# Attention of an adaLN block: pairs of heads on two row halves of TensorE, or one head at a time with wider score tiles

## What is computed

```python
mod = (silu(c) @ wmod).reshape(8, 6, 1, 1024)
sa, ca, ga, sb, cb, gb = ...                     # ga, gb kept at least 0.25 from zero
h = layernorm(x) * (1 + ca) + sa
x = x + ga * attn(h, W_qkv)                      # 16 heads of 64, 2048 tokens, softmax(q k / 8) v
h = layernorm(x) * (1 + cb) + sb
x = x + gb * ffn(h)                              # 1024 -> 4096 -> 1024, gated by silu
# ffn: activations rounded to 8 bits per token, weights to -1, 0, 1 times their mean magnitude
```

## Time and profile before

| | |
|---|---|
| median of 3 runs (lowest to highest) | 3792.73 us (3792.7 to 3797.2) |
| the profiled execution, its own time | 3794.45 us |
| span of its slowest core (core 6), first to last instruction | 3792.6 us |
| spans of the 8 cores | 3770.1 to 3792.6 us |
| mean granted clock of PE, by core | 0.697 to 0.702 |

### The profile page before, as it was taken

How to read it: one execution, slowest core, us unless ns; L and a number is a source line. 1 busy time by engine, 2 the same in 40 slices (tenths; PEclk the granted TensorE clock), 3 DMA queues, 4 the chain that set the end, 5 groups by cost and what they waited for, 6 DMA issues and landing times.

```text
span 3792.6 us, 31402 instructions; the slowest of 8 cores (3770.1 to 3792.6 us)
## 1 busy us (share of the span) xinstructions
PE 2596.1 (68%) x8072; PEld 767.5 (20%) x8156; DVE 1655.0 (44%) x2454; ACT 1194.3 (31%) x1711; POOL 243.9 (6%) x445
## 2 busy tenths in 40 slices
PE   7528745888888888888888886220856856856856
PEld 1103310111111111111111111010322322322322
DVE  0375642433233344332333443568463463464464
ACT  0100035333344433333444331234342242232232
POOL 0000001100111111100111110000000000000000
PEclk9759855666655666666565666555977977977977
DMA  6349811111111111111211111422414414414413
GB/s 215 147 147 248 247 40 38 51 32 30 40 50 51 50 50 51 39 29 33 50 51 50 50 50 57 145 89 89 145 48 141 125 46 134 124 53 127 132 53 108
DMA packets 209167, 327.47 MB, mean 86 GB/s; under 512 B 135985, under 2 KB 136242, under 8 KB 194658
## 3 DMA queue, kind: packets, MB, share of 16 engines
q1 hardware_dynamic: 167122, 226.88, 19.1%
q0 software_dynamic: 41872, 98.59, 9.7%
HBM read 289.68 MB, written 42.01 MB: 87 GB/s over the span
## 4 chain that ended last, share of the span: by engine, by line
PE 45%; DVE 22%; ACT 12%; DMA 10%; issue 8%; DVEq 1%; ACTq 1%; SPq 0%; POOL 0%; POOLq 0%
PE spsE L734 7%; PE spsO L734 7%; ACT PT L756 5%; PE avps L791 5%; PE avps L787 5%; PE dops L795 5%; PE spsE L746 4%; PE dps L1407 3%; DVE gq L1339 2%; DVE vq L1366 2%; DVE gpb L1243 2%; DVE gup L1256 2%; DVE mab L1269 2%; ACT sgb L1251 2%; DMA wc<-wqkvT 2%
## 5 line engine op out<-in xcount | busy, mean ns | idle before, releaser
L818 DVE RECIPROCAL bcsb<-bcps 128x512 bf16<-128x512 f32 x64 | 214.9, 3357 | 1018.3 <-PE bcps L811 1009.8
L756 ACT ACTIVATE PT<-spsE 128x512 bf16<-128x512 f32 x512 | 305.8, 597 | 411.5 <-PE spsO L746 386.8
L734 PE MATMUL spsE<-c8pair,onesb 1*128 1x512 bf16 x512 | 289.7, 571 | 158.3 <-ACT PT L756 123.8
L1229 PE MATMUL gps<-hA,tg 128*128 128x512 bf16 x1004 | 248.3, 388 | 189.9 <-DMA tu<-ternu 120.6
L734 PE MATMUL spsO<-c8pair,onesb 1*128 1x512 bf16 x512 | 288.4, 568 | 54.3 <-ACT PT L756 1.6
L756 ACT ACTIVATE PT<-spsO 128x512 bf16<-128x512 f32 x512 | 305.7, 597 | 48.3 <-ACT PT L756 1.5
L746 PE MATMUL spsO<-Qc,Kc 64*128 64x512 bf16 x512 | 262.0, 613 | 0.0
L746 PE MATMUL spsE<-Qc,Kc 64*128 64x512 bf16 x512 | 261.3, 611 | 0.0
L1233 PE MATMUL ups<-hA,tu 128*128 128x512 bf16 x1002 | 242.3, 382 | 1.1
L1352 PE MATMUL dps<-gq,td 128*128 128x512 bf16 x250 | 126.9, 609 | 163.3 <-DVE gq L1339 163.3
L791 PE MATMUL avps<-PT,Vc 128*64 128x512 bf16 x512 | 222.1, 434 | 0.0
(11 more groups left out here) (176 smaller groups left out, 2955.4 us busy)
## 6 DMA issues: line engine op xcount, KB each, us to landing
tg<-terng SPq DMA_DIRECT2D x128, 256.0 KB, 2.7
tu<-ternu SPq DMA_DIRECT2D x128, 256.0 KB, 3.0
td<-ternd POOLq DMA_DIRECT2D x32, 1024.0 KB, 6.4
wmb<-wmod SPq DMA_DIRECT2D x8, 2048.0 KB, 7.9
xs<-xT SPq DMA_DIRECT2D x16, 1024.0 KB, 5.8
mb<-wgT SPq DMA_DIRECT2D x8, 2048.0 KB, 10.4
mb<-wuT SPq DMA_DIRECT2D x8, 2048.0 KB, 9.8
mb<-wdT SPq DMA_DIRECT2D x8, 2048.0 KB, 9.5
```

Of the source, the lines that this page charges most:

```text
L734: p.inc(TE.matmul(sps[(par, n2)], onesb[bp:bp + 1, :], c8pair[bp:bp + 1, n2 * 512:(n2 + 1) * 512], start=True, stop=False, tile_position=( ...
L756: p.inc(S.activation(PT[par][:, kt * 1024 + n2 * 512: kt * 1024 + (n2 + 1) * 512], sps[(par, n2)], AF.Exp, scale=0.125), eS)
L818: p.inc(V.reciprocal(bcsb, bcps[:]), eV)
L1229: p.inc(TE.matmul(gps[pb], tgc[buf][:, d * 128:(d + 1) * 128], hA[:, d * T + ts0: d * T + ts0 + 512], start=(d == 0), stop=(d == NDC - 1)) ...
```

## The change

1. Attention goes head by head (16 heads, 2 halves each) instead of pair by pair. A step kt writes one PSUM tile of 128x1024, of two that alternate by step (sps0, sps1), with two one-row matmuls (from row 0 for both heads) and two of 64 rows. One exponential of 128x1024 reads it. The one-row matmul of a step waits for the exponential of two steps before.
2. After the 16 steps of a head and half follow that head's two bursts with V.
3. The rounding pieces are spread as 12 for each head and half, in steps 2 to 13; none are left for the end of a half. c8 is one row, loaded once for each head and half.
4. In `emit_ln_apply` the third step goes from DVE to ACT (Identity with scale and bias), and tscr gets a second buffer. What waited for DVE's count waits for ACT's: the first Q projection, and SP's first load of the weight means.

```diff
--- before.py
+++ after.py
@@ -277,7 +277,9 @@
     g_Rb, Rb = alloc("Rb", [128, T], F32, "right")
     g_MRb, MRb = alloc("MRb", [128, T], F32, "right")
     g_lsc, lsc = alloc("lsc", [128, 3 * 512], F32, "right")
-    g_tscr, tscr = alloc("tscr", [128, T], F32, "right")
+    g_tscr, tscr0 = alloc("tscr", [128, T], F32, "right")
+    g_tscr1, tscr1 = alloc("tscr1", [128, T], F32, "right")
+    tscr = [tscr0, tscr1]
     xs, xbt, xqt = [xs0, xs1], [xb0, xb1], [xq0, xq1]
 
     def emit_ln_stats(src_dram, S1ps, S2ps, first_wait=None):
@@ -349,6 +351,7 @@
     def emit_ln_apply(src_dram, scale_vec, shift_vec, dest_tile, Rbo, MRbo,
                       tok_rb, dtoks=None):
         use_tok = {}
+        stok = {}
         for d in range(NDC):
             buf = d % 2
             if d < 2:
@@ -361,19 +364,23 @@
                           src_dram[d * 128:(d + 1) * 128, :])
             p.wait(V, "V", dxs, tok_x)
             p.wait(V, "V", eV, tok_rb)
-            p.wait(V, "V", eV)
-            p.inc(V.tensor_mul(tscr, xs[buf], Rbo), eV)
+            if d >= 2:
+                p.wait(V, "V", eS, stok[d - 2])
+            p.wait(V, "V", eV)
+            p.inc(V.tensor_mul(tscr[buf], xs[buf], Rbo), eV)
             use_tok[d] = p.cnt[eV]
             p.wait(V, "V", eV)
-            p.wait(V, "V", eV)
-            p.inc(V.tensor_sub(tscr, tscr, MRbo), eV)
-            p.wait(V, "V", eV)
-            p.wait(V, "V", eV)
-            p.inc(V.tensor_scalar(dest_tile(d), tscr, scale_vec[:, d:d + 1],
-                                  shift_vec[:, d:d + 1], ALU.mult, ALU.add), eV)
+            p.inc(V.tensor_sub(tscr[buf], tscr[buf], MRbo), eV)
+            tok_n = p.cnt[eV]
+            p.wait(S, "S", eV, tok_n)
+            p.wait(S, "S", eS)
+            p.inc(S.activation(dest_tile(d), tscr[buf], AF.Identity,
+                               scale=scale_vec[:, d:d + 1],
+                               bias=shift_vec[:, d:d + 1]), eS)
+            stok[d] = p.cnt[eS]
             if dtoks is not None:
-                dtoks[d] = p.cnt[eV]
-        return p.cnt[eV]
+                dtoks[d] = p.cnt[eS]
+        return p.cnt[eS]
 
     with (nc.psum_tensor("S1psA", [128, T], F32) as s1t,
           nc.psum_tensor("S2psA", [128, T], F32) as s2t):
...
@@ -424,8 +432,8 @@
         wsrc, base, j = mean_plan[k]
         red_tok = mean_state["red"]
         if k == 0:
-            p.wait(Y, "Y", eV, tok_h)
-            p.wait(Y, "Y", eS)
+            p.wait(Y, "Y", eS, tok_h)
+            p.wait(Y, "Y", eV)
             p.wait(Y, "Y", eT)
         if wsrc.shape[0] == D:
             src = wsrc[j * 128:(j + 1) * 128, :]
@@ -463,7 +471,7 @@
             p.wait(TE, "T", sem_e, tok_e)
             for d in range(NDC):
                 if ec == 0:
-                    p.wait(TE, "T", eV, lnap_tok[d])
+                    p.wait(TE, "T", eS, lnap_tok[d])
                 for gq in range(4):
                     sl = slice(gq * 512, (gq + 1) * 512)
                     p.inc(TE.matmul(qkps[buf][:, sl],
...
@@ -692,19 +700,17 @@
     g_PT1, PT1 = alloc("PT1", [128, NTC * 1024], BF16, "left")
     PT = [PT0, PT1]
 
-    with (nc.psum_tensor("spsE0", [128, 512], F32) as se0,
-          nc.psum_tensor("spsE1", [128, 512], F32) as se1,
-          nc.psum_tensor("spsO0", [128, 512], F32) as so0,
-          nc.psum_tensor("spsO1", [128, 512], F32) as so1,
+    with (nc.psum_tensor("sps0", [128, 1024], F32) as s0t,
+          nc.psum_tensor("sps1", [128, 1024], F32) as s1t_,
           nc.psum_tensor("avps0", [128, 512], F32) as av0t,
           nc.psum_tensor("avps1", [128, 512], F32) as av1t,
           nc.psum_tensor("dops", [1, 512], F32) as dot,
           nc.psum_tensor("bcps", [128, 512], F32) as bct):
-        sps = {(0, 0): se0[:], (0, 1): se1[:], (1, 0): so0[:], (1, 1): so1[:]}
+        sps = [s0t[:], s1t_[:]]
         avps = [av0t[:], av1t[:]]
         dops = dot[:]
         bcps = bct[:]
-        exp_sbuf_tok = {(0, 0): 0, (0, 1): 0, (1, 0): 0, (1, 1): 0}
+        exp_sbuf_tok = [0, 0]
         pt_avdone = [0, 0]
         av_evac_tok = [0, 0]
         do_read_tok = 0
@@ -715,73 +721,63 @@
         p.wait(TE, "T", eV, tok_qk_v)
         p.wait(TE, "T", eV, tok_negC)
         p.wait(TE, "T", eS, tok_qk_s)
+        c8tok = {}
         p.wait(Y, "Y", "dc8", tok_c8)
-        p.dma(Y, "Y", "dc80", c8pair[0:1, :], C8h[0:1, 0:1024])
-        c8row_tok = {(0, 0): p.dma(Y, "Y", "dc80", c8pair[64:65, :],
-                                   C8h[1:2, 0:1024])}
-        for c in range(NH // 2):
+        c8row_tok = {(0, 0): p.dma(Y, "Y", "dc80", c80, C8h[0:1, 0:1024])}
+        for h in range(NH):
+            c = h // 2
+            par = h % 2
+            bp = 64 * par
+            cb = c80
             for half in range(2):
-                tok_c8row = c8row_tok[(c, half)]
+                hb = half
+                tok_c8row = c8row_tok[(h, half)]
                 for kt in range(NTC):
-                    lhsTs = {0: Kc[0:64, c * T + kt * 128: c * T + (kt + 1) * 128],
-                             1: Kc[64:128, c * T + kt * 128: c * T + (kt + 1) * 128]}
+                    sp = kt % 2
+                    p.wait(TE, "T", eS, exp_sbuf_tok[sp])
+                    if kt == 0:
+                        p.wait(TE, "T", "dc80", tok_c8row)
+                    lhsT = Kc[bp:bp + 64, c * T + kt * 128: c * T + (kt + 1) * 128]
                     for n2 in range(2):
-                        for par in range(2):
-                            p.wait(TE, "T", eS, exp_sbuf_tok[(par, n2)])
-                            if kt == 0 and n2 == 0:
-                                p.wait(TE, "T", "dc80", tok_c8row)
-                            bp = 64 * par
-                            p.inc(TE.matmul(sps[(par, n2)],
-                                            onesb[bp:bp + 1, :],
-                                            c8pair[bp:bp + 1,
-                                                   n2 * 512:(n2 + 1) * 512],
-                                            start=True, stop=False,
-                                            tile_position=(bp, 0)), eT)
+                        cs = n2 * 512
+                        p.inc(TE.matmul(sps[sp][:, n2 * 512:(n2 + 1) * 512],
+                                        onesb[0:1, :], cb[0:1, cs:cs + 512],
+                                        start=True, stop=False), eT)
                     if kt == NTC - 1:
                         tok_lastr1 = p.cnt[eT]
                     for n2 in range(2):
                         q0 = c * T + half * 1024 + n2 * 512
-                        for par in range(2):
-                            bp = 64 * par
-                            p.inc(TE.matmul(sps[(par, n2)], lhsTs[par],
-                                            Qc[bp:bp + 64, q0:q0 + 512],
-                                            start=False, stop=True,
-                                            tile_position=(bp, 0)), eT)
-                        tok_sc2 = p.cnt[eT]
-                        for par in range(2):
-                            p.wait(S, "S", eT, tok_sc2)
-                            if kt == 0 and n2 == 0:
-                                p.wait(S, "S", eT, pt_avdone[par])
-                            p.wait(S, "S", eS)
-                            p.inc(S.activation(
-                                PT[par][:, kt * 1024 + n2 * 512:
-                                        kt * 1024 + (n2 + 1) * 512],
-                                sps[(par, n2)], AF.Exp, scale=0.125), eS)
-                            exp_sbuf_tok[(par, n2)] = p.cnt[eS]
-                    if 1 <= kt <= 15:
+                        p.inc(TE.matmul(sps[sp][:, n2 * 512:(n2 + 1) * 512],
+                                        lhsT, Qc[bp:bp + 64, q0:q0 + 512],
+                                        start=False, stop=True,
+                                        tile_position=(bp, 0)), eT)
+                    tok_sc = p.cnt[eT]
+                    p.wait(S, "S", eT, tok_sc)
+                    if kt == 0:
+                        p.wait(S, "S", eT, pt_avdone[hb])
+                    p.wait(S, "S", eS)
+                    p.inc(S.activation(PT[hb][:, kt * 1024:(kt + 1) * 1024],
+                                       sps[sp], AF.Exp, scale=0.125), eS)
+                    exp_sbuf_tok[sp] = p.cnt[eS]
+                    tok_lastsc = p.cnt[eT]
+                    if 2 <= kt <= 13:
                         emit_tern_piece()
                 tok_exp_all = p.cnt[eS]
-                nc_, nhalf = (c, 1) if half == 0 else (c + 1, 0)
-                if nc_ < NH // 2:
+                nh, nhalf = (h, 1) if half == 0 else (h + 1, 0)
+                if nh < NH:
                     p.wait(Y, "Y", eT, tok_lastr1)
-                    p.dma(Y, "Y", "dc80", c8pair[0:1, :],
-                          C8h[2 * nc_:2 * nc_ + 1,
-                              nhalf * 1024:(nhalf + 1) * 1024])
-                    c8row_tok[(nc_, nhalf)] = p.dma(
```

(24 more changed lines are left out.)

## The result

The changed kernel takes 3714.17 us (median of 8 runs, 3703.17 to 3726.54), the one before 3793.14 us (median of 8, 3784.6 to 3809.63): ratio 0.9789, 95% interval 0.9768 to 0.9811. The profiled execution took 3735.63 us, 21 above the median.

The account below looks back on a forecast made before the run. PE and ACT taking turns in attention's score steps was taken as the bound. Terms -23 + 16 - 7 - 13 = -27 against 3794.45 gave 3767, 3766 by the median; own range 3715 to 3815, outer bounds 3690 to 3850.

Parts of the forecast that it names:

- part 1: Attention score steps: 1.93 us a step set by PE's own stream, -23 us over 16 rounds.
- PE's not waiting for ACT: Score steps: PE no longer waits, up to a 1.56 us exponential; rival that turn-taking stays, about 3979, chance 0.05.
- The open change: Score step, 64-row to one-row matmul, not in the trace: 0.57 us taken, bounds 0.43 and 0.77.
- the dear change: Rival, score steps: 64-row to one-row change costs over 0.62 us; at 0.77 the sum is 3870; chance 0.14.
- odd heads overlap: Rival, score steps: odd heads' one-row and score matmuls run together, -210 us, 3558; chance 0.03.
- The score stretches: Attention scores: 32.4 us a head and half, 64.7 for two against 66.1 for the pair, -23 us in all.
- part 2: Bursts with V: one starting after scores at the low clock comes twice a round, +16 us, bounds nothing to +88.
- part 3: Rounding pieces, reciprocals, stores and c8 row beside attention: costed at nothing; a late row would stop PE at 32 borders.
- part 4: Layer norm 1: third step off DVE makes a chunk 4.8 us instead of 6.25, -7 us.
- part 5: End of attention: no pieces left, so POOL loads x earlier and layer norm 2 starts sooner, -13 us (-11 to -16).
- The clock rival: Score stretch: PE without pauses reaches 2.4 GHz, ACT sets steps of about 1.2 us, about 3390; chance 0.10.
- The rule on packing: Score matmuls on separate row groups run concurrently; by this rule alone giving that up costs +205 us, sum 3979.

Follow-up runs that it names:

- z1_pause: Changed kernel with PE held before each score stretch until the multiplication behind the last burst is done; 1.0281 of the kernel before.
- x3_order: Kernel before with only the burst order changed, both of the even head and then both of the odd; 0.9997 of the kernel before.
- y4_exp512: Changed kernel with each 128x1024 exponential split into two of 128x512; 0.9866 of the kernel before.
- y3: Changed kernel with both the one-row and the 64-row score matmuls made into 128-row ones; 3320.91 us, 0.874 of the kernel before.
- y1: Changed kernel with only the one-row score matmuls made into 128-row ones by zero padding; 0.9632 of the kernel before.

## Why the prediction was right in sign and wrong in size

Between the forecast's -27 and the -85 of these stages lie 58 us: 26 in the score stretches, 26 in the bursts, 5 at the end of attention and 1 in the layer norm.

- *The step* (part 1) was right in its sum, 1.93 us, in the exponential, 1.023, in PE's not waiting for ACT, and in the 2.05 us (mean) from the last score matmul to the first burst. The open change, 64-row to one-row, is 0.56 us (0.96 less 0.40), where 0.57 was taken: the dear change did not come, nor did odd heads overlap. That the sum fits so well is in part luck: the other change costs 0.56, not 0.51, and each of the two followers 0.40, not 0.427, and these errors of 0.05 cancel.
- *The score stretches* (part 1, "a head and half is 16 x 1.93 + 1.48 = 32.4 us"), forecast -23 and measured -49: **a term that was mis-sized.** The sum charged every step at 1.2 GHz. A stretch takes 29.60 us from first to last matmul, not 15 x 1.93 + 1.37 = 30.3: 0.7 x 32 = 22 us. z1_pause shows the cause, the full clock that the last burst leaves. In the kernel before it was hidden: 119 of its 128 stretches also begin at 1.00, but the next step's first matmul waits there for ACT's exponentials, and its pair of stretches measured 67.2 us with the spreading, as the forecast had it (66.1 + 1.0).
- *The bursts* (part 2, "Once a round becomes twice: +1.0 us a round, +16 us"): **the step that failed, in sign.** The effect named is there: the odd head's burst that now follows scores costs 13.22 instead of 12.18, the forecast's +1.0. But the other three places were held constant, and they moved too: even first -0.63, even second -1.55, odd second +0.51; the four give -0.63, x 16 = -10, below the stated bounds (nothing to +88). The even head's second burst before, then its two after (windows, columns as above):

```profile
1024.00:1030.32 6.32, 5.33 (x17) 2.29 (x17) 4.05 (x2) 0.59 (x1) 0.00 (x0) 0.73 0.00 0
...
1284.71:1290.82 6.11, 5.11 (x16) 2.19 (x17) 0.00 (x0) 0.59 (x1) 0.00 (x0) 0.75 0.00 0
1291.84:1296.48 4.64, 3.64 (x17) 1.74 (x17) 4.04 (x2) 0.59 (x1) 0.00 (x0) 1.00 0.00 0
```

  By the granted clock at a burst's first matmul, on all cores, the odd head's first burst enters at 0.50 instead of 1.00. The even head's first burst enters at 0.50 and its second at 1.00 in both kernels, so what shortened these two is when the level rises or falls inside them: the second shown keeps 1.00 to its end, where the one before fell on the way (0.73). x3_order shows that the order alone shifts time among the bursts; z1_pause and y4_exp512 show that the sum is another with other things ahead of a burst (593 to 622 us in all with the same matmuls). Why the even bursts got faster is not settled: when the clock rises or falls within a burst was not brought under control in any run.
- Both misses have to do with the granted clock at the borders, of which the change makes 32 out of 16. The forecast followed it from scores into a burst alone, and took one level for the rest (0.50 in scores, one length for every burst amid others). That it is carried from a burst into scores is shown; that the bursts' 26 us come from what they hand to each other is argued, not shown.
- *Nothing beside it* (part 3): right; PE waits for the c8 row once, 8.8 us ahead of the first stretch as in the kernel before, and at none of the 31 borders behind it.
- *Layer norm* (part 4): -7.7 for -7; on the core above chunk 1 came at 224.97, not 221.1, because chunk 0 already began later in this execution (212.80; 209.09 on the core of the earlier trace rows). From chunk 0 to chunk 1 it is 12.17 us instead of 11.25, the 0.8 that was forecast, and the pace behind it was 4.79.
- *End of attention* (part 5): -18.4 for -13. The gap behind the last multiplication went from 17.43 to 2.45 us on the cores shown, -15, in the stated -11 to -16. The load of x took 6.2 us there (2294.67 to 2300.89). The upper bound of 10.7 was misread: the wait that ends at 2360.21 in the earlier trace rows is one for a store of rounded weights (DMA ternd<-tto); this load had landed at 2356.56, in 7.1 us. The other 3 us lie later in the stage and are not explained.
- *The clock rival* failed as forecast: with PE busy for 27.12 of 27.12 us the clock is 0.50. The table in the Trainium skill, TensorE: Matmul & The Clock Gate, on why this matters has the full clock for a TensorE kept busy; for matmuls of 1 and 64 rows this trace disagrees, for 128 rows y3 agrees. The rival's price of a step was good: 1.2 us was worked out at the full clock, y3's is 1.18 ((1018.18 - 1015.83) / 2). Its 3390 us for the whole kernel left out that the bursts get shorter too.
- *The rule on packing* (the Trainium skill, TensorE: Matmul & The Clock Gate, Part 3) is true of the pairs before, but what it saves was smaller than what the turn-taking cost.

## What to carry to other kernels

Where a stage's clock differs from its neighbour's, count the borders and ask which level each side enters with; a step priced at one clock is right only once it is settled. A stretch of short-row matmuls at the half clock is worth more as a target than its schedule: here the reordering gave 79 us, and zero-padding the same matmuls to 128 rows some 400 more (0.9789 - 0.874 = 0.105 of 3793). What the change did to transfers and queues was forecast from rows to within some 5 us (-7.7 for -7, -18.4 for -13).

## What the runs showed of the hardware that was not expected

- Matmuls of 1 and 64 rows, without a gap between them, kept the clock at 0.50, and every stretch that was entered at 1.00 fell to it, the one shown in its first step (0.53 in 1297.94 to 1298.88).
- With 128-row and 64-row matmuls in turn (y1) the stretch has two outcomes, 1.00 throughout (62 of 256) or 0.50 after a short start; a start at 1.00 is needed for the first and is not enough.
- Going between a one-row and a 64-row matmul costs 0.16 us more than staying with one kind (0.56 and 0.40 in the settled stretch). The Trainium skill, TensorEngine Tiling (Array Packing), Key Properties, says that a switch of the tiling mode drains the engine. The cost would fit that; whether it is this drain, no run shows. Where all have 128 rows (y3) four in a row at the half clock stand 0.43 us apart (0.85 a pair) with no such cost.
